# Gate logits of a token's own row: from nine rows by tokens, turned, to tokens by nine columns

## The chip, the cores and the metric

The kernel runs on one core of a Trainium2 chip, as one launch. The metric is device time in microseconds (us). Three runs of the kernel before gave 445.64, 446.63 and 454.53 us, median 446.63 us.

## The reference

The input x has 128 sequences of 64 tokens with 128 channels, so 8192 tokens. Two residual blocks are computed:

```
x = x + tanh(g_xattn) * attention(layernorm(x), ctx, ctx)     # 16 heads of 8, softmax over 64 keys, W_o
x = x + tanh(g_ffn)   * experts(layernorm(x))                 # top 1 of 8 experts
experts(y): logits = (y @ w_red) @ normalised(wg).T           # [tokens, 8]
            idx = argmax, score = max of softmax(logits)
            o = (gelu(y @ W1[idx] + b1[idx]) @ W2[idx] + b2[idx]) * score
```

The kernel does not wait for the finished attention to compute the logits from it. Layer normalisation is linear in the row apart from its scale, and so the logits of a token are the sum of a share of its own row (the subject of the change) and a share of the attention's output, times a scale. With `wc`, a matrix of 128 channels by nine columns (eight experts' weights, mean taken out, and 1/128 for the mean), the own share is xnormed @ wc, times the row's standard deviation.

## The kernel before, in words

**Tiling.** The tokens are cut into 64 units of 128 tokens, and the units into 16 chunks of four. One loop of 76 slots (`for k in range(SLOTS)`, k = 4s + j) is written out on each engine, and each slot serves one unit at each stage of the attention: `scores1` (L1167) for the maximum over keys, four units behind; `scores2` (L1150, L1157) ten behind; values (L1232) eleven behind; the output matrix (L1244) twelve behind. Each slot has also one of four pieces of work on chunk s, by j:

- j = 0: four turns of the normalised x (L1319) and four of the context (L1266), one turn of `xwT` (L1325), one turn of the maxima `mx` (L1327); on ScalarE the copies `xT` (L629), `cT` (L575) and `mS` (L663);
- j = 1: keys (L1273); on VectorE `x_logits`, which scales the own logits into `XR` (L811);
- j = 2: the first two units of `x_logits` on TensorE (L1256), then queries (L1337, 512 columns);
- j = 3: the other two units of L1256, then values of the context (L1344); on ScalarE the copies `V` (L656), and `xwT` (L668).

In the slot k = 7 (s = 1, j = 3) all four units of chunk 0 are done in one L1256 block. The first softmax comes in slot 10.

**The order of the work** is that of the program on each engine, tied by semaphores. A slot's loop runs over three engines: TensorE's `scores1` of unit k - 4 is reduced by VectorE (L1012, in two halves); ScalarE's two exponentials `PT` of slot k (L614, L616) wait for the halves; TensorE's L1150 of the next slot waits for both exponentials (`pt_ok`). GpSimd makes `MD` from `mS` (L459) and then sends finished rows with their logits to a list in HBM by indirect DMAs (L416, 64 of them). SyncE's queue loads x, context and weights and spreads keys and queries.

**The expert part** (from about 299 us) takes 71 tiles of 128 rows from that list, with two layers on TensorE (L1286, L1384) and an indirect DMA by GpSimd for each tile's output (L489).

**The own logits before.** `x_logits` (L1249) multiplies `wc` padded to 32 columns, held stationary, with the 128 turned rows of a unit moving. Unit u of a chunk lands on partitions 32u to 32u + 31 of the PSUM bank `m2`, so the four units of a chunk use four column groups of the array. ScalarE copies the block to `xwT`, TensorE turns it into another part of `m2`, and VectorE reads 8 of each 32 columns with the tokens on the partitions.

Of the kernel before, what the change touches and what calls it, by code (L numbers as in the profile page):

```python
# [6 lines left out]
ACT = mybir.ActivationFunctionType  # L7
# [6 lines left out]
P = 128  # L14
# [6 lines left out]
CU = 4  # L21
CT = CU * P
NC = N // CT
# [5 lines left out]
NE = 8  # L29
# [5 lines left out]
NX = NE + 1  # L35
# [28 lines left out]
def gated_block(nc, x, ctx_in, g_xattn, g_ffn, W_q, b_q, W_k, b_k, W_v, b_v, W_o, b_o, w_red, wg, W1, b1, W2, b2, out):  # L64
    es = ExitStack()
    with es:
        def sb(name, shape, dt=F32):
            return es.enter_context(nc.sbuf_tensor(name, shape, dt))
# [4 lines left out]
        def sem(name):  # L73
            return es.enter_context(nc.semaphore(name))
# [7 lines left out]
        ident = sb("ident", [P, P])  # L82
# [10 lines left out]
        wt = sb("wt", [P, 2, P])  # L93
# [9 lines left out]
        wgT = sb("wgT", [GD, NE])  # L103
        nrm = sb("nrm", [NE, 4])
        wmean = sb("wmean", [GD, 2])
        wc = sb("wc", [P, 32])
        w1 = sb("w1", [P, NE, HID])
        w2 = sb("w2", [P, NE, HH, D])
        w1l = sb("w1l", [P, NE, HID])
# [15 lines left out]
        gve, dev2, bmean = sb("gve", [P, CU]), sb("dev2", [P, D]), sb("bmean", [P, 2])  # L125
        xn = sb("xn", [P, CU, D])
        xT = [sb(f"xT{i}", [P, CT]) for i in range(2)]
        cT, xwT = sb("cT", [P, CT]), sb("xwT", [P, P])
        Qf = sb("Qf", [P, CT])
        qb = [sb(f"qb{i}", [P, CT], BF16) for i in range(2)]  # L130
        kb = sb("kb", [P, CT], BF16)
# [37 lines left out]
        pv = pb("pv", [P, 512])  # L169
        rec = pv[:, 400:416].rearrange("p (a l) -> p a l", l=2)  # L170
        m0, m1, m2 = (pb(n, [P, 512]) for n in ("m0", "m1", "m2"))
# [22 lines left out]
        s1_ps, mxa_ok, mx_ok, mT_ps, mS_ok, s2_ps, pt_ok = (sem(n) for n in ("s1_ps", "mxa_ok", "mx_ok", "mT_ps", "mS_ok", "s2_ps", "pt_ok"))  # L194
        pv_ps, val_ps, tv_ok, rec_ok, nv_ok, ot_ok, x1_ok = (
            sem(n) for n in ("pv_ps", "val_ps", "tv_ok", "rec_ok", "nv_ok", "ot_ok", "x1_ok"))
        gsq_ok, gve_ok, g_pay, xw_ps, xwT_ok, xwt_ps, lgx_ok = (
            sem(n) for n in ("gsq_ok", "gve_ok", "g_pay", "xw_ps", "xwT_ok", "xwt_ps", "lgx_ok"))
        wt_ps, wt_ok, woc_ps, wox_ok, std_ok, peak_ok, lead_ok = (
            sem(n) for n in ("wt_ps", "wt_ok", "woc_ps", "wox_ok", "std_ok", "peak_ok", "lead_ok"))  # L200
        diff_ok, ex_ok, oh_ok, cnt_ps, cnt_rd, pos_ok, gate_ok = (
# [292 lines left out]
        def _(act):  # L494
# [110 lines left out]
            for k in range(SLOTS):  # L605
                s, j = k // CU, k % CU
                n = k - LAG2
                if 0 <= n < NU:
                    act.wait_ge(s2_ps, n + 1)
                    act.wait_ge(mxa_ok, min(k - LAG1 + 1, NU))  # L610
                    if n >= 2:
                        act.wait_ge(pv_ps, pv_turn(n - 2 + LAGV))
                    pt = PT[n % 2][:, :, :].rearrange("p (t i) q -> p t (i q)", t=RT)
                    nc.scalar.activation(pt[:, 0:2], sc[:, 0:2, 256:512], ACT.Exp)  # L614
                    act.wait_ge(mx_ok, min(k - LAG1 + 1, NU))
                    nc.scalar.activation(pt[:, 2:4], sc[:, 2:4, 256:512], ACT.Exp).then_inc(pt_ok, 1)  # L616
                if k == 7:
                    gate_weights_end()
                if k == 0:
                    turned_context(0)  # L620
                    permuted(wq, wqp)
                    permuted_biases()
                    bias_columns()
                    keys(0)
                if j == 0 and s < NC:
                    act.wait_ge(xT_ps, s + 1)
                    if s >= 2:
                        act.wait_ge(xw_ps, s - 1)
                    nc.scalar.activation(xT[s % 2][:, :], m0[:, :], ACT.Copy).then_inc(xT_sb, 1)  # L629
                if k == 0:  # L630
                    keys_turned(0)
                    act.wait_ge(w_in, 16 * NWI)
                    nc.scalar.activation(tg[:, :], gx[:, :], ACT.Tanh)
                    nc.scalar.activation(tgf[:, :], gf[:, :], ACT.Tanh).then_inc(tg_ok, 1)
                if j == 0 and 1 <= s < NC:
                    turned_context(s)
                if j == 1 and 1 <= s < NC:
                    keys(s)
                    keys_turned(s)
                if j == 2 and s < NC:  # L640
                    act.wait_ge(q_ps, s + 1)
                    if s >= 2:
                        act.wait_ge(s1_ps, CU * (s - 1))
                    nc.scalar.activation(qb[s % 2][:, :], m0[:, :], ACT.Identity, bias=b16[:, 0:1], scale=ISC).then_inc(qb_ok, 1)
                    if s >= 1:
                        act.wait_ge(qd_in[(s - 1) % 3], 16 * HI * ((s - 1) // 3 + 1))
                    nc.scalar.activation(Qf[:, :], m0[:, :], ACT.Identity, bias=b16[:, 0:1], scale=ISC).then_inc(qf_ok, 1)
                if j == 3 and s < NC:
                    act.wait_ge(v_ps, s + 1)
                    if s < 3:  # L650
                        act.wait_ge(zero_p, s + 1)
                    else:
                        act.wait_ge(pv_ps, pv_turn(CU * (s - 3) + CU - 1 + LAGV))
                    for p in range(2):
                        r = slice(S * p, S * p + S)
                        i = nc.scalar.activation(V[s % 3][r, :, :, DK * p:DK * p + DK].rearrange("p u h d -> p (u h) d"),  # L656
                                                 m1[r, :].rearrange("p (a d) -> p a d", d=DK), ACT.Copy)
                    i.then_inc(v_ok, 1)
                if j == 0 and 2 <= s < NC + 2:
                    act.wait_ge(mT_ps, s - 1)  # L660
                    if s >= 4:
                        act.wait_ge(md_ok, s - 3)
                    nc.scalar.activation(mS[s % 2][:, :], m2[:, 0:P], ACT.Copy, scale=-1.0).then_inc(mS_ok, 1)  # L663
                if j == 3 and 1 <= s < NC + 1:
                    act.wait_ge(xw_ps, s)
                    if s >= 2:
                        act.wait_ge(xwt_ps, s - 1)
                    nc.scalar.activation(xwT[:, :], m2[:, P:2 * P], ACT.Copy).then_inc(xwT_ok, 1)  # L668
                if k == 5:
                    reduced_weights()  # L670
                if k == 6:
                    turned_weights()
                if k == 10:
                    output_logits()
                if k - LAGO - 1 >= 0:
                    squares(k - LAGO - 1)
                if k in gate_at:
                    gate_exp(gate_at[k])
                if k == SLOTS - 3:
                    nc.scalar.activation(warm[:, :], one[:, :], ACT.Gelu)  # L680
                if k == SLOTS - 3:
                    f_turned(0)
                if k == SLOTS - 2:
                    f_gelu(0)
                    f_turned(1)
# [11 lines left out]
        def _(dve):  # L697
# [14 lines left out]
            nc.vector.memset(mx[0][:, :, :], 0.0)  # L712
            nc.vector.memset(mx[1][:, :, :], 0.0)
            nc.vector.memset(nrm[:, 3:4], 0.5)
            nc.vector.memset(wc[:, NX:32], 0.0)
            nc.vector.memset(wc[:, NE:NX], 1.0 / D)
            for i in range(2):
                nc.vector.memset(fx[i][:, D - 1:D], 1.0)
# [86 lines left out]

            def x_logits(c):

                dve.wait_ge(xwt_ps, c + 1)
                dve.wait_ge(mS_ok, c + 1)
                dve.wait_ge(std_ok, c + 1)  # L810
                nc.vector.tensor_tensor(XR[:, CU * c:CU * c + CU, D:D + NE],  # L811
                                        m2[:, 2 * P:3 * P].rearrange("p (u r) -> p u r", u=CU)[:, :, 0:NE],
                                        std[c % 3][:, :].rearrange("p (u o) -> p u o", o=1).to_broadcast([P, CU, NE]),
                                        ALU.mult).then_inc(lgx_ok, 1)

# [291 lines left out]
        def _(pe):  # L1107
# [23 lines left out]
            def setup_logits():  # L1131
                pe.wait_ge(wt_ok, 1)
                pe.wait_ge(wc_ok, 1)
                for a in range(2):
                    i = nc.tensor.matmul(pv[:, NX * a:NX * a + NX], wt[:, a, :], wc[:, 0:NX], start=True, stop=True,
                                         skip_group_check=True)
                i.then_inc(woc_ps, 1)

# [110 lines left out]
            def x_logits(c, units):  # L1249

                pe.wait_ge(xT_sb, c + 1)
                pe.wait_ge(wc_ok, 1)
                if c >= 1:
                    pe.wait_ge(lgx_ok, c)
                for u in units:
                    i = nc.tensor.matmul(m2[32 * u:32 * u + 32, P:2 * P], wc[:, :], xT[c % 2][:, P * u:P * u + P],  # L1256
                                         start=True, stop=True, skip_group_check=True)
                if CU - 1 in units:
                    i.then_inc(xw_ps, 1)
# [32 lines left out]
            for k in range(SLOTS):  # L1292
# [28 lines left out]
                    if s >= 1:  # L1321
                        context(s)
                if j == 0 and 2 <= s < NC + 2:
                    pe.wait_ge(xwT_ok, s - 1)
                    nc.tensor.transpose(m2[:, 2 * P:3 * P], xwT[:, :], ident[:, :]).then_inc(xwt_ps, 1)  # L1325
                    pe.wait_ge(mx_ok, CU * (s - 1))
                    nc.tensor.transpose(m2[:, 0:P], mx[s % 2][:, :, :].rearrange("p t r -> p (t r)"),  # L1327
                                        ident[:, :]).then_inc(mT_ps, 1)
# [99 lines left out]
```

## Time and profile before

| | |
|---|---|
| median of 3 runs | 446.63 us |
| lowest, highest | 445.64, 454.53 us |
| span of the profiled execution | 445.2 us, 15463 instructions |
| TensorE matmul busy | 354.6 us (80%), 5630 |
| TensorE weight loads busy | 257.0 us (58%), 5630 |
| VectorE busy | 288.0 us (65%), 1031 |
| ScalarE busy | 241.2 us (54%), 604 |
| GpSimd busy | 260.1 us (58%), 413 |
| mean granted TensorE clock | 0.897 of 2.4 GHz |

The profiled execution has no time of its own beside its span; the span lies 0.4 us under the lowest run and 1.4 us under the median. In the profile PE is TensorE's matmuls, PEld its weight loads, DVE is VectorE, ACT ScalarE, POOL GpSimd. L1256 is line 1256 of the kernel. "issue" is idle time in which the engine waited for nothing that the profile shows, and "remote" is a wait whose releaser it doesn't find.

### The profile page before, as it was taken

Reading aid. Unit: us, or ns where it says so; the run is one execution under the profiler, and the core shown is the slowest. Engines: PE = TensorE matmul, PEld = TensorE weight load, DVE = VectorE, ACT = ScalarE, POOL = GpSimd, SP = SyncE. Lnnn points to the kernel's source line nnn. Section 1 sums busy time; section 2 is a strip of 40 time slices with the busy share of each in tenths; the row PEclk is TensorE's granted clock in tenths of the full one; section 3 lists DMA queues with packets and bytes.
Section 4 is the critical chain, followed back from the end, with each engine's and each line's share of the span. In section 5 each row is a group of like instructions: output and inputs, shape, how many; then the busy total and the mean of one; then the engine's idle time right before and its main releaser. Section 6 shows DMA issues by size and latency. Waiting matters only on the chain.

```text
span 445.2 us, 15463 instructions
## 1 busy us (share of the span) xinstructions
PE 354.6 (80%) x5630; PEld 257.0 (58%) x5630; DVE 288.0 (65%) x1031; ACT 241.2 (54%) x604; POOL 260.1 (58%) x413
## 2 busy tenths in 40 slices
PE   4778999999979889889876776768559888878880
PEld 2346566676636556566543545557448667766770
DVE  6968798989848766868853657565435454445440
ACT  3667889888938676777762524443212333333330
POOL 6558465556866945865854444446564656556652
PEclk9989999999969897998995967579685999999997
DMA  5245444333232131221110111401134222222110
GB/s 124 86 134 132 114 122 121 110 99 106 73 93 77 58 100 35 93 76 35 52 54 28 45 35 49 113 28 41 51 98 115 84 83 81 79 69 77 49 36 4
DMA packets 47157, 34.01 MB, mean 76 GB/s; under 512 B 9800, under 2 KB 42955, under 8 KB 47083
## 3 DMA queue, kind: packets, MB, share of 16 engines
q1 hardware_dynamic: 42440, 23.90, 19.5%
q0 software_dynamic: 4352, 9.00, 6.0%
q8 instruction: 46, 0.75, 0.7%
q14 instruction: 27, 0.22, 0.2%
q10 hardware_dynamic: 292, 0.13, 0.1%
HBM read 17.13 MB, written 10.04 MB: 61 GB/s over the span
## 4 chain that ended last, share of the span: by engine, by line
PE 59%; DVE 14%; issue 12%; ACT 4%; another core or an unknown queue 4%; SPq 2%; DMA 1%; POOL 1%; DVEq 1%; POOLq 0%; ACTq 0%
PE sc L1286 10%; PE m L1384 8%; PE pv L1232 8%; PE sc L1157 5%; PE pv L1244 4%; PE m L1337 4%; PE m L1344 3%; PE sc L1167 3%; PE sc L1150 3%; DVE mx L1012 3%; PE m L1256 2%; PE sc L1278 2%; PE m L1381 2%; PE m L1273 2%
## 5 line engine op out<-in xcount | busy, mean ns | idle before, releaser
L1012 DVE TENSOR_REDUCE mx<-sc 128x8 f32<-128x512 f32 x128 | 82.2, 683 | 45.5 <-PE sc L1167 23.6
L489 POOL DMA_INDIRECT out<-fo,rr x71 | 72.0, 1014 | 58.7 <-DVE fo L1083 39.4
L1232 PE MATMUL pv<-PT,V 128*32 128x64 f32 x2048 | 55.7, 233 | 25.0 <-issue 20.0
L416 POOL DMA_INDIRECT records<-XR,pos x64 | 63.4, 990 | 17.0 <-issue 16.8
L1083 DVE SCALAR_TENSOR_TENSOR fo<-m,rr 128x128 f32<-128x128 f32 x71 | 24.8, 350 | 66.3 <-PE m L1384 55.2
L614 ACT ACTIVATE PT<-sc 128x512 f32<-128x512 f32 x64 | 38.1, 596 | 53.3 <-issue 27.5
L1232 PEld LDWEIGHTS pv<-PT,V 128*32 128x32 f32 x2048 | 39.0, 115 | 39.3 <-issue 32.2
L1286 PE MATMUL sc<-fxT,w1s 128*128 128x128 f32 x284 | 50.2, 304 | 5.6 <-DVE w1s L991 3.0
L1384 PE MATMUL m<-w,fgT 128*128 x284 | 52.9, 313 | 0.1
L459 POOL TENSOR_TENSOR MD<-mS,imask 128x256 bf16<-128x256 bf16 x16 | 9.8, 612 | 70.4 <-ACT mS L663 70.4
L602 ACT ACTIVATE fgT<-sc 128x256 f32<-128x256 f32 x71 | 27.2, 383 | 41.7 <-PE sc L1286 29.5
L1286 PEld LDWEIGHTS sc<-fxT,w1s 128*128 128x128 f32 x284 | 41.0, 208 | 11.6 <-issue 7.8
L1157 PE MATMUL sc<-Qd,kT 32*128 32x128 f32 x1024 | 46.3, 288 | 1.2 <-issue 1.2
L596 ACT ACTIVATE fxT<-sc 128x128 f32<-128x128 f32 x70 | 19.4, 277 | 49.8 <-PE sc L1278 25.2
L1384 PEld LDWEIGHTS m<-w,fgT 128*128 128x128 f32 x284 | 40.5, 206 | 2.2 <-issue 0.2
L1157 PEld LDWEIGHTS sc<-Qd,kT 32*128 32x128 f32 x1024 | 39.4, 201 | 2.8 <-issue 2.7
L1021 DVE STREAM_TRANSPOSE TV<-pv 128x256 f32<-128x256 f32 x64 | 28.3, 441 | 18.6 <-remote 13.1
L616 ACT ACTIVATE PT<-sc 128x512 f32<-128x512 f32 x64 | 38.2, 597 | 0.0
L1278 PE MATMUL sc<-ident,fx 128*128 128x128 f32 x70 | 21.4, 306 | 13.3 <-DVE fx L975 9.2
L1244 PE MATMUL pv<-wox,OT 128*128 128x137 f32 x108 | 29.0, 350 | 1.4 <-issue 1.4
L1150 PEld LDWEIGHTS sc<-MD,usel 32*128 32x128 bf16 x256 | 6.5, 92 | 36.7 <-ACT PT L616 23.7
L543 ACT ACTIVATE dev<-XR 128x128 f32<-128x128 f32 x64 | 25.8, 404 | 1.5 <-issue 1.3
(216 smaller groups left out, 735.3 us busy)
## 6 DMA issues: line engine op xcount, KB each, us to landing
rr<-records SPq DMA_DIRECT2D x71, 72.0 KB, 1.9
XC<-in_x SPq DMA_DIRECT2D x16, 256.0 KB
C<-in_ctx SPq DMA_DIRECT2D x16, 256.0 KB
Qd<-Qf SPq DMA_DIRECT2D x64, 64.0 KB
Kd<-kb SPq DMA_DIRECT2D x64, 32.0 KB
w<-in_L_ffn_W SPq DMA_DIRECT2D x16, 128.0 KB, 2.9
out<-fo,rr POOLq DMA_INDIRECT x71
w1l<-in_L_ffn_W SPq DMA_DIRECT2D x8, 128.0 KB, 3.9
```

What stands on the lines that cost most here:

```text
L416: nc.gpsimd.indirect_dma_start(out=records, out_offset=bass.IndirectOffsetOnAxis(ap=pos[:, u:u + 1], axis=0), in_=XR[:, u, :], in_offset=N ...
L489: nc.gpsimd.indirect_dma_start(out=out_rows, out_offset=bass.IndirectOffsetOnAxis(ap=rr[q][:, R_ID:R_ID + 1].bitcast(U32), axis=0), in_=fo ...
L614: nc.scalar.activation(pt[:, 0:2], sc[:, 0:2, 256:512], ACT.Exp)
L616: nc.scalar.activation(pt[:, 2:4], sc[:, 2:4, 256:512], ACT.Exp).then_inc(pt_ok, 1)
L1012: nc.vector.tensor_reduce(mx[c % 2][:, t:t + 2, HI * u:HI * u + HI], sc[:, t:t + 2, 0:256].rearrange("p t (i k) -> p t i k", i=HI), AX_X, ...
L1021: nc.vector.transpose(TV[:, :, :].rearrange("p a r -> p (a r)"), pv[:, 0:2 * P]).then_inc(tv_ok, 1)
L1157: m = nc.tensor.matmul(sc[:, t, 256 + P * b:256 + P * b + P].rearrange("p (i q) -> p i q", i=2), kT[c % 3][r, u, b, :, :].rearrange("r l k ...
L1232: last = nc.tensor.matmul(pv[32 * t:32 * t + 32, P * b:P * b + P].rearrange("p (h i q) -> p i h q", h=2, i=2)[:, i], vf[:, at:at + 32], PT ...
L1244: last = nc.tensor.matmul(attn_out(k), OT[no % 2][:, :], wox[:, :], start=True, stop=True, skip_group_check=True)
L1278: nc.tensor.transpose(rows_turned(k), fx[k % 2][:, :], ident[:, :]).then_inc(f_tr, 1)
L1286: i = nc.tensor.matmul(sc[:, 2 + p, P * m:P * m + P], w1s[p][:, P * m:P * m + P], fxT[p][:, :], start=True, stop=True, skip_group_check=True)
L1384: i = nc.tensor.matmul(o, fgT[p][:, m, :], w2[:, bass.ds(e, 1), m, :].rearrange("p o c -> p (o c)"), start=False, stop=(m == HH - 1), skip ...
```

## The change

`x_logits` on TensorE swaps the operands: the 128 turned rows of a unit are the stationary operand, and the nine columns of `wc` move. The result has the tokens on the partitions at once, nine columns for each unit, side by side in `m2`. ScalarE's copy to `xwT`, TensorE's turn of it, their two semaphores and the padding of `wc` go. VectorE's `x_logits` reads the new place and waits for the matmuls (`xw_ps`).

```
-        wc = sb("wc", [P, 32])
+        wc = sb("wc", [P, NX])                      # NX = 9
...
-        cT, xwT = sb("cT", [P, CT]), sb("xwT", [P, P])
+        cT = sb("cT", [P, CT])
...
-                if j == 3 and 1 <= s < NC + 1:      # ScalarE
-                    act.wait_ge(xw_ps, s)
-                    if s >= 2:
-                        act.wait_ge(xwt_ps, s - 1)
-                    nc.scalar.activation(xwT[:, :], m2[:, P:2 * P], ACT.Copy).then_inc(xwT_ok, 1)
...
-            nc.vector.memset(wc[:, NX:32], 0.0)
...
-                dve.wait_ge(xwt_ps, c + 1)          # VectorE, x_logits
+                dve.wait_ge(xw_ps, c + 1)
...
-                                        m2[:, 2 * P:3 * P].rearrange("p (u r) -> p u r", u=CU)[:, :, 0:NE],
+                                        m2[:, P:P + CU * NX].rearrange("p (u r) -> p u r", u=CU)[:, :, 0:NE],
...
-                    i = nc.tensor.matmul(m2[32 * u:32 * u + 32, P:2 * P], wc[:, :], xT[c % 2][:, P * u:P * u + P],
+                    i = nc.tensor.matmul(m2[:, P + NX * u:P + NX * u + NX], xT[c % 2][:, P * u:P * u + P], wc[:, :],
                                          start=True, stop=True, skip_group_check=True)
...
-                    pe.wait_ge(xwT_ok, s - 1)       # TensorE, j = 0
-                    nc.tensor.transpose(m2[:, 2 * P:3 * P], xwT[:, :], ident[:, :]).then_inc(xwt_ps, 1)
```

## Rows read from the trace of the kernel before

**Rows 1.** The page's chain that ended last: shares of the span by engine.
```profile
PE 59%; DVE 14%; issue 12%; ACT 4%; another core or an unknown queue 4%; SPq 2%; DMA 1%; POOL 1%; DVEq 1%; POOLq 0%; ACTq 0%
```

**Rows 2.** Two stages: length, busy of PE, PEld, DVE, ACT, POOL, PEclk, DMA, GB/s.
```profile
33.00:122.00 89.00, 85.23 (x2043) 59.68 (x2047) 79.54 (x272) 77.99 (x179) 56.02 (x136) 1.00 0.40 109
122.00:299.00 177.00, 141.43 (x2717) 94.95 (x2714) 118.15 (x421) 101.22 (x245) 103.21 (x156) 0.84 0.20 61
```

**Rows 3.** Waits of TensorE's weight loads: total us, times, longest us.
```profile
PEld pv L1232 <- issue: 32.2, 47, 2.7
PEld sc L1150 <- ACT PT L616: 23.7, 36, 1.8
```

**Rows 4.** Timeline of weight loads, a j = 2 slot: start us, us, what, [idle before].
```profile
73.81 0.30 PEld L1244 LDWEIGHTS pv<-wox,OT 128*128 128x128 f32 x2
74.24 0.14 PEld L1256 LDWEIGHTS m<-xT,wc 128*32 128x32 f32 x4
74.58 0.30 PEld L1337 LDWEIGHTS m<-xT,wqp 128*128 128x128 f32 x2 [0.20 <-issue]
75.64 0.10 PEld L1150 LDWEIGHTS sc<-MD,usel 32*128 32x128 bf16 x4 [0.76 <-ACT PT L616]
```

**Rows 5.** Timeline of VectorE and ScalarE: second exponentials of two slots, one reduction.
```profile
74.95 0.61 ACT L616 ACTIVATE PT<-sc 128x512 f32<-128x512 f32 x1
...
80.05 1.29 DVE L1012 TENSOR_REDUCE mx<-sc 128x8 f32<-128x512 f32 x2 [0.56 <-PE sc L1167]
...
81.37 0.60 ACT L616 ACTIVATE PT<-sc 128x512 f32<-128x512 f32 x1
```

**Rows 6.** Timeline of weight loads, end of a j = 0 slot.
```profile
80.49 0.30 PEld L1244 LDWEIGHTS pv<-wox,OT 128*128 128x128 f32 x2
80.71 0.48 PEld L1319 LDWEIGHTS m<-ident,xn 128*128 128x128 f32 x4
...
81.59 0.14 PEld L1325 LDWEIGHTS m<-ident,xwT 128*128 128x128 f32 x1
81.70 0.14 PEld L1327 LDWEIGHTS m<-ident,mx 128*128 128x128 f32 x1
82.02 0.10 PEld L1150 LDWEIGHTS sc<-MD,usel 32*128 32x128 bf16 x4 [0.18 <-ACT PT L616]
```

**Rows 7.** Timeline of weight loads: two matmuls of nine columns (setup), full clock.
```profile
30.91 0.53 PEld L1135 LDWEIGHTS pv<-wc,wt 128*128 128x128 f32 x4
31.45 0.12 PEld L1167 LDWEIGHTS sc<-Kd,qb 32*64 32x64 bf16 x8
```

**Rows 8.** Timeline of weight loads, a j = 3 slot.
```profile
77.14 0.30 PEld L1244 LDWEIGHTS pv<-wox,OT 128*128 128x128 f32 x2
...
77.91 1.01 PEld L1344 LDWEIGHTS m<-wv,cT 128*64 128x64 f32 x32 [0.20 <-issue]
```

**Rows 9.** Timeline of weight loads in setup at half clock: one-column matmuls.
```profile
9.58 0.92 PEld L1112 LDWEIGHTS m<-one,browp 1*128 1x128 f32 x4 [1.50 <-issue]
10.52 0.50 PEld L1319 LDWEIGHTS m<-ident,xn 128*128 128x128 f32 x3
```

**Rows 10.** Timeline of weight loads in slot 7: four units in one block.
```profile
26.35 0.23 PEld L1256 LDWEIGHTS m<-xT,wc 128*32 128x32 f32 x8 [0.30 <-issue]
26.97 0.40 PEld L1344 LDWEIGHTS m<-wv,cT 128*64 128x64 f32 x6 [0.38 <-issue]
```

**Rows 11.** The chain of waits after slot 7's block: start us, us, what.
```profile
27.04 1.93 PE m L1344 x32
...
29.60 0.60 ACT V L656
```

**Rows 12.** Timeline of ScalarE in two j = 3 slots with a gate's exponential.
```profile
106.81 0.28 ACT L668 ACTIVATE xwT<-m 128x128 f32<-128x128 f32 x1
106.98 0.39 ACT L543 ACTIVATE dev<-XR 128x128 f32<-128x128 f32 x1
...
208.33 0.28 ACT L668 ACTIVATE xwT<-m 128x128 f32<-128x128 f32 x1
```

More of the change, by code:

```diff
@@ L196, in gated_block @@
             sem(n) for n in ("pv_ps", "val_ps", "tv_ok", "rec_ok", "nv_ok", "ot_ok", "x1_ok"))
-        gsq_ok, gve_ok, g_pay, xw_ps, xwT_ok, xwt_ps, lgx_ok = (
-            sem(n) for n in ("gsq_ok", "gve_ok", "g_pay", "xw_ps", "xwT_ok", "xwt_ps", "lgx_ok"))
+        gsq_ok, gve_ok, g_pay, xw_ps, lgx_ok = (sem(n) for n in ("gsq_ok", "gve_ok", "g_pay", "xw_ps", "lgx_ok"))
         wt_ps, wt_ok, woc_ps, wox_ok, std_ok, peak_ok, lead_ok = (
@@ L1134, in setup_logits @@
                 for a in range(2):
-                    i = nc.tensor.matmul(pv[:, NX * a:NX * a + NX], wt[:, a, :], wc[:, 0:NX], start=True, stop=True,
+                    i = nc.tensor.matmul(pv[:, NX * a:NX * a + NX], wt[:, a, :], wc[:, :], start=True, stop=True,
                                          skip_group_check=True)
```

## The prediction, made before the changed kernel was run

> **What bounds the kernel now.** I read the chain of waits first. TensorE holds 59% of it [rows 1], so what the change takes from TensorE and ScalarE counts only where that work ends a wait. Next, the busy time by stage: from 33 to 122 us TensorE computes 85 of 89 us at full clock, and from 122 to 299 us 141 of 177 us at a mean clock of 0.84 [rows 2]. The second stage is long because of the largest wait, in which no engine holds TensorE up: L1232 stands 32.2 us on "issue" [rows 3]. The change has no part in L1232.
>
> Then the waits at the slot's edge. A slot begins with L1150, which waits for the second exponential L616 of the slot before, and in 36 of the 64 slots the weight loads end their idle time on just that [rows 3]. The timeline shows the loop behind it. The reduction takes 1.29 us from 80.05, to 81.34. L616 starts at 81.37 and ends at 81.97 [rows 5], and L1150 loads at 82.02 [rows 6], 0.05 us later. So the j = 0 slot, which holds L1325, ends on VectorE's reduction and one exponential, though TensorE looks full in it. The j = 2 slot is nearly as tight: L616 ends at 75.56 [rows 5], L1150 loads at 75.64 [rows 4]. With a release of 0.05 us, only 0.03 us is left between TensorE's pace and the loop's.
>
> **The change part by part.**
>
> *The block of two units in a j = 2 slot (14 slots, s = 2 to 15).* Counted from L1244's first load. Now L1337 loads at 74.58 - 73.81 = 0.77 us [rows 4]. Of this 0.43 us passes before L1256 loads, while behind the same L1244 a block with the full 128 x 128 tile loads after 80.71 - 80.49 = 0.22 us [rows 6]: passing from a tile of 128 columns to one of 32 costs the difference. The new form is the full tile. Its price is its weight loads: the setup has the same form, two float32 matmuls with 128 x 128 stationary and nine columns moving, and takes 31.45 - 30.91 = 0.54 us for four loads, the passage to another tile included [rows 7]. The pace of 128 x 128 float32 loads is (81.59 - 80.71) / 8 = 0.11 us [rows 6], over four of L1319 and four of L1266. So L1337 would load at 0.22 + 4 x 0.11 = 0.66 us, 0.10 us sooner (0.11 before rounding). But the loop allows 0.03. The bounds are 14 x 0.03 = 0.4 and 14 x 0.10 = 1.4 us; some of these slots end later than the loop wants, behind the holes in L1232, and keep the whole. I take -0.6, near the lower end, since rows 3 put most slot edges on the exponential.
>
> *The block of two units in a j = 3 slot (14 slots).* Now L1344 loads 77.91 - 77.14 = 0.77 us after L1244 [rows 8]. New: 0.22 + 0.54 = 0.76, since L1344 has another tile and the passage stays. I take 0; bounds -0.01 and +0.01 a slot.
>
> *The block of four units in slot 7.* This is where the old form was cheap. Its units lie in four column groups, and eight loads and matmuls pass in 26.97 - 26.35 = 0.62 us, at half clock [rows 10]. The new form has one tile for all and must take eight full loads in turn. At half clock four 128-column loads with one-column matmuls take 10.52 - 9.58 = 0.94 us [rows 9], 0.215 each without the end. Eight are 0.94 + 4 x 0.215 = 1.80 us, so +1.2 us. At full clock it would be 0.54 + 4 x 0.11 - 0.62 = +0.4, the lower bound. It is on the path: L1344, then the copy V (L656), then the context's turns follow it in the chain [rows 11].
> The Trainium skill, in "TensorE: Matmul & The Clock Gate" (Part 3, Packing small matmuls), says that matmuls of 32 output rows in different column groups run at once, three of them 2.38 times as fast; by that rule alone undoing the packing is a loss, as the 0.62 us for eight show here, but the j = 2 and j = 3 blocks had only two groups side by side.
>
> *L1325, the turn.* It takes 81.70 - 81.59 = 0.11 us [rows 6] on TensorE, 16 times. 15 lie in slots that end on the exponential: 0, with a bound of -1.6 us if the loop weren't there. The first lies in the setup on the path between V and slot 10: -0.1.
>
> *L668, ScalarE's copy.* The work behind it starts 106.98 - 106.81 = 0.17 us later [rows 12]. In a usual slot the exponential waits for the reduction anyway: 0. In three slots, from 106.81 to 208.33 us, ScalarE also has a gate's exponential and goes from V to the exponentials without a pause [rows 12], the first and the last of them, so 3 x 0.17 = -0.5.
>
> *VectorE.* `x_logits` reads the same 32 elements a partition, waits for an event that comes a slot earlier, and also for `mS` as before: 0. Behind it stand VectorE's gate steps and the next reduction, which lose nothing. One memset in the setup: 0, it ran beside the first loads. GpSimd's MD waits for `mS`, behind `xT` and `cT` on ScalarE: unmoved, and so are the sends. No DMA is added or moved, on SyncE's queue or GpSimd's.
>
> **Sum:** +1.2 - 0.1 - 0.6 - 0.5 = 0.0 us against the span of 445.2, which lies 1.4 us under the median. The same on the median: **446.6 us**. The profile's best reading of the edit is that it gives back in many slots what it costs once.
>
> **The rivals.**
>
> *TensorE's time counts everywhere.* If the slots are bound by TensorE rather than by the loop (it is 96% busy up to 122 us), the saving is 14 x 0.10 + 16 x 0.11 + 0.5 = 3.7 us; less 1.2 in slot 7 is -2.5, and 444.1 us. For it: the chain's share. Against: L1150's waits [rows 3, 5]. Chance 0.17.
>
> *The holes in the supply move.* L1232 stands 32.2 us on "issue", 47 times [rows 3]. The changed kernel has 32 fewer array instructions and its slots shift against GpSimd's sends. If a third of the holes goes, the time is 446.6 - 10.7 = 436 us; as easily a few are added, to about 452. Nothing in the edit pushes either way. 0.12, of which 0.07 for the side below.
>
> *Slower, by the clock.* The clock is 0.84 in the second stage [rows 2] and at half in slot 7. In slot 7 the array now streams nine columns where it streamed 128. If the return to 2.4 GHz comes later there, L1344 (1.93 us at half clock [rows 11], its loads 1.01 at full [rows 8]), the turns and the first scores take about 1.5 us more: 448 us, chance 0.2. That case decides from slot 7, as soon as the granted clock stays at half beyond L1344's matmuls. If it also drops the mean of the second stage, the price is larger: 177 us at 0.84 hold 177 x 0.16 x 2 = 57 us at half clock; at 0.78 it would be 78, and 21 more at half clock cost at most half of that, 10 us: with the 1.5 us of slot 7 that is 458 us, chance 0.06.
> The skill's page "TensorE: Matmul & The Clock Gate" (Part 1, The HAM clock gate) says that the default clock is the low one and that array activity lifts it, which would count against short matmuls between long loads; whether loads count, it doesn't say and no row here shows.
>
> *The change doesn't do what it says:* both the copy and the turn are gone from the text. What can fail is the load pace, if reading `xT` as stationary stalled behind ScalarE's reads: 28 blocks by one more load of 0.11 are +3.1 us, 449.7. Chance 0.05.
>
> **How the numbers follow.** The forecast of no change has 0.40, the rivals 0.17, 0.12, 0.20, 0.06 and 0.05. The range 439 to 452.5 us takes in the first rival, the small clock case, the load pace, the bounds (-1.4 to +1.2) and the spread of the runs shown, and leaves out a large move of the holes and the large clock case. 2% of 446.6 is 8.9 us, about what can be told from no change here. Beyond it lie only the lower case of the holes (0.07) and a little of the first rival together with it, so faster 0.09; the large clock case and a bad move of the holes, so slower 0.08; within 0.83.
>
> **What would show each step.** In the changed profile: L1256 loads of 128 x 128 at 0.11 us a pace; L1337 loading about 0.66 us after L1244; L1150 of the next slot still 0.05 us after L616 in j = 0 and now in j = 2 slots too; the slot 7 block about 1.8 us long if the clock is at half, and the first L1150 about 1.1 us later; that lag worked off by some 0.3 to 0.4 us until 122 us, and the rest behind it. The sum is wrong if the first L1150 isn't later, if j = 0 slots get shorter, or if the second stage's clock or its "issue" time differs by more than a few us.

## The result, and the profile after

The changed kernel took **453.34 us** (median of 4 runs, 450.57 to 456.07), the kernel before 447.60 beside it (median of 4). The ratio is 1.0145, 95% interval 1.0091 to 1.0199. Timed a second time among the experiments it gave 1.0124 (1.0044 to 1.0203). A ratio here compares only the runs within 1.5% of the fastest of their own kernel. The change is a loss of some 1.3%, 5 to 6 us, where I had forecast none, and 453.34 lies above the range.

One caution first. The two profiles are 8.8 us apart, and that is more than the change. A span is some 2 us shorter than the time of its run (454.0 for 456.07 us). The 77 runs of the kernel before that the ratios below use have a mean time of 447.5 us (443.1 to 450.9) and a mean span of 445.1, so the profile of before, with 445.2, is an ordinary one. The four runs of the changed kernel have a mean span of 451.2 us, and the one profiled, with 454.0, is the longest of them. Some 3 us of the 8.8 are the luck of that run.

The page of the changed kernel, busy time by engine, the clock, and the chain by engine:

```profile
span 454.0 us, 15399 instructions
PE 368.4 (81%) x5614; PEld 279.4 (62%) x5614; DVE 289.7 (64%) x1030; ACT 239.4 (53%) x588; POOL 259.9 (57%) x413
PEclk9968999999965898997995757588585999989896
PE 52%; issue 13%; DVE 12%; ACT 6%; another core or an unknown queue 4%; POOL 1%; DVEq 0%; POOLq 0%; ACTq 0%
```

The 16 copies are gone from ScalarE (588 for 604) and the 16 turns from TensorE (5614 for 5630), as the diff says. Weight loads are busy 22 us longer. The first digits of the clock row are the first surprise: the third and fourth slice are 6 and 8, where they were 8 and 9 before.

The same stages as in [rows 2]: length, busy time of PE, PEld, DVE, ACT and POOL, granted clock, DMA share, GB/s.

```profile
33.00:122.00 89.00, 85.44 (x2011) 62.36 (x2014) 78.56 (x266) 75.64 (x168) 54.84 (x135) 0.98 0.38 104
122.00:299.00 177.00, 146.44 (x2709) 106.09 (x2698) 116.26 (x411) 99.31 (x234) 102.22 (x155) 0.79 0.20 62
```

The second stage runs at 0.79 where it ran at 0.84.

**The steady part went as worked out.** Weight loads of a j = 2, a j = 3 and a j = 0 slot of the changed kernel (L1237 is the old L1244, L1249 the block in question, L1328 and L1335 the old L1337 and L1344, L1143 the old L1150, L1318 the old L1327):

```profile
76.80 0.30 PEld L1237 LDWEIGHTS pv<-wox,OT 128*128 128x128 f32 x2
77.03 0.53 PEld L1249 LDWEIGHTS m<-wc,xT 128*128 128x128 f32 x4
77.48 0.30 PEld L1328 LDWEIGHTS m<-xT,wqp 128*128 128x128 f32 x2
78.60 0.10 PEld L1143 LDWEIGHTS sc<-MD,usel 32*128 32x128 bf16 x4 [0.82 <-ACT PT L615]
...
80.10 0.30 PEld L1237 LDWEIGHTS pv<-wox,OT 128*128 128x128 f32 x2
80.33 0.53 PEld L1249 LDWEIGHTS m<-wc,xT 128*128 128x128 f32 x4
80.88 1.01 PEld L1335 LDWEIGHTS m<-wv,cT 128*64 128x64 f32 x32
81.96 0.10 PEld L1143 LDWEIGHTS sc<-MD,usel 32*128 32x128 bf16 x4
...
84.56 0.14 PEld L1318 LDWEIGHTS m<-ident,mx 128*128 128x128 f32 x1
84.99 0.10 PEld L1143 LDWEIGHTS sc<-MD,usel 32*128 32x128 bf16 x4 [0.28 <-ACT PT L615]
```

L1328 loads 0.68 us after L1237 (0.66 forecast, 0.77 in [rows 4]); L1335 0.78 us after (0.76 forecast, 0.77 in [rows 8]). From the L1143 at 78.60 to that at 81.96 are 3.36 us, to the next 3.03. Over the slots 13 to 36 the median j = 0 slot takes 3.03 us before and 3.04 after, the median j = 2 slot 3.34 and 3.30, the median j = 3 slot 3.35 and 3.36. Without the turn the idle time before L1143 is 0.28 us where it was 0.18 in [rows 6], and its releaser is still the exponential: the turn's 0.1 us became a wait.

**The start did not.** Weight loads of the changed kernel from slot 7 to slot 10 (L1160 is the old L1167, L1128 the old L1135):

```profile
26.35 1.78 PEld L1249 LDWEIGHTS m<-wc,xT 128*128 128x128 f32 x8 [0.21 <-issue]
28.16 1.79 PEld L1335 LDWEIGHTS m<-wv,cT 128*64 128x64 f32 x32
...
32.40 0.98 PEld L1128 LDWEIGHTS pv<-wc,wt 128*128 128x128 f32 x4
33.41 0.14 PEld L1160 LDWEIGHTS sc<-Kd,qb 32*64 32x64 bf16 x8
...
35.78 0.11 PEld L1143 LDWEIGHTS sc<-MD,usel 32*128 32x128 bf16 x4 [1.50 <-DVE mx L1005]
```

The block takes 28.16 - 26.35 = 1.81 us, the 1.80 of the forecast, against 0.62 [rows 10]. But the setup block L1128 takes 1.01 us here and 0.54 before [rows 7], so the array is still at half clock, and the first scores load at 35.78 instead of 33.2 us. The granted clock shows it. Windows from 26 us, the same columns, of the kernel before:

```profile
26.00:30.00 4.00, 3.87 (x60) 2.64 (x60) 2.77 (x9) 1.23 (x4) 2.12 (x5) 0.59 0.18 62
30.00:34.00 4.00, 3.31 (x48) 2.23 (x48) 2.78 (x10) 2.86 (x7) 1.11 (x2) 1.00 0.55 132
34.00:38.00 4.00, 3.00 (x74) 1.59 (x68) 3.62 (x10) 3.32 (x8) 4.00 (x11) 1.00 0.86 203
```

and of the changed kernel:

```profile
26.00:30.00 4.00, 3.93 (x48) 3.69 (x48) 2.25 (x8) 0.24 (x2) 2.11 (x5) 0.54 0.21 76
30.00:34.00 4.00, 4.00 (x34) 3.12 (x31) 1.63 (x5) 2.55 (x5) 0.51 (x1) 0.50 0.73 138
34.00:38.00 4.00, 4.00 (x35) 2.04 (x36) 2.58 (x8) 2.06 (x4) 2.52 (x7) 0.68 0.54 149
```

In both profiles the clock has just fallen to 1.2 GHz when the block begins at 26.35 us. Before, it is back at 2.4 GHz (1.00) from 30 us on; after, it stays at 0.50 until beyond 34. TensorE counts as busy in the trace throughout: 3.93 of 4 us, then 4.00 of 4.

**And a collision behind it.** The last of VectorE's five steps on the expert bias, the reduction behind it, GpSimd's constants (the first and the last of a run of 22 memsets), and the exponential that waits, in slot 11 of the changed kernel:

```profile
40.32 2.20 DVE L815 CAST bhl<-br 128x8 bf16<-128x8 f32 x1
40.62 0.22 POOL L430 MEMSET tri<- 128x128 bf16 x1
40.64 1.89 DVE L1005 TENSOR_REDUCE mx<-sc 128x8 f32<-128x512 f32 x2
...
42.38 0.12 POOL L438 MEMSET ebase<- 128x1 f32 x1
42.64 0.60 ACT L613 ACTIVATE PT<-sc 128x512 f32<-128x512 f32 x1 [2.25 <-DVE mx L1005]
```

The cast of eight elements takes 2.20 us and ends at 42.52, with GpSimd's run of memsets. Its siblings take 0.4 us. The two halves of the reduction, which start at 40.64, take 1.89 us where they take 1.27 behind the same cast before, and the exponential L613 starts only at 42.64, behind them. The Trainium skill, in "SBUF — State Buffer" (Terms), says that VectorE and GpSimd arbitrate for one pair of ports, held for a whole instruction, and that the loser blocks; that fits these rows in kind, but the cast here ends with the whole run and not with one memset. The next slot start, 4.6 us after the last, shows the price: the same slot took 3.45 us before. It happened in both profiles of the changed kernel and in that of e9 below, and in no profile in which the clock was back by 34 us.

### The profile page after: what moved, and what is told of

Same layout as the page of the kernel before. It is cut to its first block, busy times and chain, and to the rows that moved or that the text cites. A ratio compares the mean times of both kernels' runs of the same rounds, so it can differ in the third digit from the quotient of the medians.

```text
span 454.0 us, 15399 instructions
## 1 busy us (share of the span) xinstructions
PE 368.4 (81%) x5614; PEld 279.4 (62%) x5614; DVE 289.7 (64%) x1030; ACT 239.4 (53%) x588; POOL 259.9 (57%) x413
## 4 chain that ended last, share of the span: by engine, by line
PE 52%; issue 13%; DVE 12%; ACT 6%; another core or an unknown queue 4%; POOL 1%; DVEq 0%; POOLq 0%; ACTq 0%
PE sc L1279 9%; PE m L1375 7%; PE pv L1225 7%; PE sc L1150 6%; PE m L1335 3%; PE m L1328 3%; PE pv L1237 3%; PE sc L1143 3%; DVE mx L1005 3%; PE sc L1160 3%; PE m L1249 2%; ACT PT L615 2%; ACT PT L613 2%; PE sc L1271 2%
## 5 line engine op out<-in xcount | busy, mean ns | idle before, releaser
L1225 PE MATMUL pv<-PT,V 128*32 128x64 f32 x2048 | 56.8, 240 | 22.6 <-issue 18.3
L613 ACT ACTIVATE PT<-sc 128x512 f32<-128x512 f32 x64 | 38.3, 598 | 57.4 <-issue 28.0
L1225 PEld LDWEIGHTS pv<-PT,V 128*32 128x32 f32 x2048 | 40.6, 120 | 36.8 <-issue 29.4
L1279 PE MATMUL sc<-fxT,w1s 128*128 128x128 f32 x284 | 52.0, 311 | 6.5 <-issue 3.0
L1375 PE MATMUL m<-w,fgT 128*128 x284 | 54.7, 320 | 0.1
L1150 PE MATMUL sc<-Qd,kT 32*128 32x128 f32 x1024 | 49.7, 303 | 1.3 <-issue 1.3
L1279 PEld LDWEIGHTS sc<-fxT,w1s 128*128 128x128 f32 x284 | 42.5, 215 | 12.5 <-issue 7.2
L595 ACT ACTIVATE fxT<-sc 128x128 f32<-128x128 f32 x70 | 19.4, 277 | 49.5 <-PE sc L1271 34.9
L1150 PEld LDWEIGHTS sc<-Qd,kT 32*128 32x128 f32 x1024 | 42.9, 214 | 2.5 <-issue 2.4
L1375 PEld LDWEIGHTS m<-w,fgT 128*128 128x128 f32 x284 | 42.2, 213 | 2.5 <-issue 0.2
L615 ACT ACTIVATE PT<-sc 128x512 f32<-128x512 f32 x64 | 38.2, 597 | 0.0
L1143 PEld LDWEIGHTS sc<-MD,usel 32*128 32x128 bf16 x256 | 6.6, 92 | 38.9 <-ACT PT L615 27.3
L1237 PE MATMUL pv<-wox,OT 128*128 128x137 f32 x108 | 28.8, 350 | 1.3 <-issue 1.3
L1143 PE MATMUL sc<-MD,usel 32*128 32x256 bf16 x256 | 20.0, 302 | 9.4 <-ACT PT L615 7.7
```

Source lines behind the costliest of these rows:

```text
L1143: nc.tensor.matmul(sc[:, t, 256:512].rearrange("p (b i q) -> p i b q", b=2, i=2), usel[r, u, :, :].rearrange("r l k -> r (l k)"), MD[c % 2 ...
L1150: m = nc.tensor.matmul(sc[:, t, 256 + P * b:256 + P * b + P].rearrange("p (i q) -> p i q", i=2), kT[c % 3][r, u, b, :, :].rearrange("r l k ...
L1225: last = nc.tensor.matmul(pv[32 * t:32 * t + 32, P * b:P * b + P].rearrange("p (h i q) -> p i h q", h=2, i=2)[:, i], vf[:, at:at + 32], PT ...
L1237: last = nc.tensor.matmul(attn_out(k), OT[no % 2][:, :], wox[:, :], start=True, stop=True, skip_group_check=True)
L1279: i = nc.tensor.matmul(sc[:, 2 + p, P * m:P * m + P], w1s[p][:, P * m:P * m + P], fxT[p][:, :], start=True, stop=True, skip_group_check=True)
L1375: i = nc.tensor.matmul(o, fgT[p][:, m, :], w2[:, bass.ds(e, 1), m, :].rearrange("p o c -> p (o c)"), start=False, stop=(m == HH - 1), skip ...
```

## The experiments

Each ratio is to runs of the kernel before on the same chip. "Half clock" is the time at 1.2 GHz of a run, (1 - mean granted clock) x 2 x span, meaned over the runs in the ratio; for the kernel before it is 100.6 us at a mean clock of 0.887. The last column gives the mean time of the runs in the ratio and that of all runs (three, of 483, 908 and 1463 us, are in no figure). The ratio is as recorded and not the quotient of these means.

| chunk 0 (slot 7) | other chunks | else | ratio (95%) | half clock, us | mean us, in the ratio / all |
|---|---|---|---|---|---|
| old | old | | 1 | 100.6 | 447.5 / 448.8 |
| new | new, 9 columns | the change | 1.0145 (1.0091 to 1.0199) | 117.1 | 453.3 / 453.3 |
| new | new, 9 | again | 1.0124 (1.0044 to 1.0203) | 114.6 | 453.0 / 455.1 |
| old | new, 9 | e1 | 1.0033 (0.9979 to 1.0087) | 109.5 | 449.1 / 449.1 |
| old | new, 9 | e11 | 0.9995 (0.9947 to 1.0044) | 108.2 | 447.7 / 449.4 |
| new | old | e2 | 1.0069 (1.0026 to 1.0113) | 106.4 | 450.1 / 450.9 |
| new, 96 columns | new, 96 | e3 | 1.0045 (1.0009 to 1.0081) | 103.8 | 449.9 / 449.9 |
| new, 48 | new, 48 | e9 | 1.0065 (1.0022 to 1.0108) | 109.5 | 450.5 / 451.7 |
| old | new, 96 | e6 | 0.9948 (0.9898 to 0.9998) | 96.2 | 444.4 / 447.5 |
| old | new, 96 | e12 | 0.9950 (0.9889 to 1.0010) | 96.0 | 445.6 / 447.6 |
| new | new, 9 | turn and copy kept idle, e8 | 1.0083 (1.0033 to 1.0132) | 107.9 | 451.2 / 452.7 |
| new | new, 9 | split in slot 12, e7 | 1.0007 (0.9965 to 1.0049) | 106.7 | 449.6 / 452.1 |
| new | new, 9 | split in slot 14, e4 | 1.0073 (1.0031 to 1.0115) | 112.7 | 450.8 / 450.8 |
| old | new, 96 | split in slot 12, e10 | 0.9981 (0.9943 to 1.0020) | 104.4 | 447.4 / 447.9 |

**1. The old form in slot 7 alone (e1, and again as e11).** Theory A puts the loss in the start, theory B in the number of columns that the array streams in every chunk. The code here and below is shortened, with numbers in place of names; lines with + and - are against the changed kernel, if nothing else is said.

```
 def x_logits(c, units):
     for u in units:
+        if c == 0:   # column groups, wc padded to 32; ScalarE copies, TensorE turns, for this chunk alone
+            matmul(m2[32 * u:32 * u + 32, P:2 * P], wc[:, 0:32], xT[c % 2][:, P * u:P * u + P])
+        else:
             matmul(m2[:, P + 9 * u:P + 9 * u + 9], xT[c % 2][:, P * u:P * u + P], wc[:, 0:9])
```

> The new form for chunks 1 to 15, the old form (column groups, copy, turn) for chunk 0 alone, so slot 7 has its short block back. Theory A (the loss is the start: slot 7's serial loads and what follows from them): the first softmax slot starts at 33.2 us again, ratio to before 0.997 to 1.002. Theory B (the array streams fewer columns in every chunk and the clock stays low longer in the second stage): the start is regained, 2 to 3 us, but the half-clock time between slots 37 and 73 stays 15 us or more over the 55 of before and the ratio is 1.006 to 1.012.

> The same kernel as in the first experiment (chunk 0 old, chunks 1 to 15 with nine columns), again, on one chip with the next. If the width sets the clock in the steady part: 1.001 to 1.006 and 5 us or more at half clock above the kernel with 96 columns. If not: the two agree in both.

Measured 1.0033 and 0.9995, and in the two profiles the first scores load at 32.86 and 34.21 us. The start is most of the loss: 1.2% goes with one block of one slot. The half-clock time of 108 to 110 us stays 8 to 9 over the kernel before, and in the profiles that between slots 37 and 73 is 63 us where it was 55. Theory B forecast at least 15 us more between those slots. The new form of the other chunks saves nothing that can be seen: 449.1 and 447.7 us are on average 1.0 us over the kernel before.

**2. The new form in slot 7 alone (e2).**

The lines stand against the kernel before, as a sketch.

```
+        if c >= 1:   # as before
             matmul(m2[32 * u:32 * u + 32, P:2 * P], wc[:, 0:32], xT[c % 2][:, P * u:P * u + P])
+        else:
+            matmul(m2[:, P + 9 * u:P + 9 * u + 9], xT[c % 2][:, P * u:P * u + P], wc[:, 0:9])
```

> The kernel before, with the new form in chunk 0 alone. Theory A: nearly the whole loss, 1.008 to 1.014, with the clock returning at 36 us and not at 29. Theory B: only the start's loss, 1.004 to 1.007, second stage as before.

1.0069: the block's 1.2 us alone would be 1.0027, the lower end of the interval. In its profile the clock is at 0.50 from 26 to 30 and 0.52 from 30 to 34 us. This was theory B's figure in my expectation. The start alone costs 2.7 us here (450.1 against 447.5), and less than the 4.7 us that it is worth where the other chunks have nine columns (453.1 against 448.5). The two parts by themselves, 2.7 and 1.0 us, make 3.7 of the 5.7 us of the change. Each of these differences is uncertain by 1 to 2 us.

**3. More columns moving (e3 with 96, e9 with 48).** The stationary operand and the number of loads stay; only the moving operand is wider, and what it adds is never read.

```
-        wc = sb("wc", [P, 9])
+        wc = sb("wc", [P, 96])        # columns 9 to 95: a constant
...
-            matmul(m2[:, P + 9 * u:P + 9 * u + 9], xT[...], wc[:, 0:9])
+            matmul(m2[:, P + 96 * u:P + 96 * u + 96], xT[...], wc[:, 0:96])
```

> The new form in every chunk, but 96 columns move instead of 9 (the other 87 hold a constant and are not read), so the array streams longer behind the same weight loads of 0.11 us. If streaming decides the clock (theory B): half-clock time falls to that of before, the clock returns at 29 us in slot 7, ratio 1.000 to 1.005. If it is the serial loads and the shift of the holes (theory A): no difference to the changed kernel, 1.010 to 1.016.

> The new form with 48 columns moving in every chunk, between 9 (1.0124, clock 0.870) and 96 (1.0045, clock 0.884). If the streamed columns set the clock, it lies between them: clock 0.874 to 0.882, ratio 1.006 to 1.011. If the 96 columns only moved the phase, it is like either end by chance.

Work that nobody reads makes the kernel faster: 1.0045 for 1.0124 and 1.0145 with 96, 1.0065 with 48. Half-clock time goes down with the columns: 115 to 117 us for 9, 109.5 for 48, 103.8 for 96. Start of the kernel with 96 columns, weight loads, and its window from 30 us:

```profile
26.42 1.78 PEld L1268 LDWEIGHTS m<-wc,xT 128*128 128x128 f32 x8 [0.34 <-issue]
28.37 1.79 PEld L1357 LDWEIGHTS m<-wv,cT 128*64 128x64 f32 x32 [0.17 <-issue]
...
32.62 0.53 PEld L1143 LDWEIGHTS pv<-wc,wt 128*128 128x128 f32 x4
33.17 0.12 PEld L1175 LDWEIGHTS sc<-Kd,qb 32*64 32x64 bf16 x8
```

```profile
30.00:34.00 4.00, 4.00 (x38) 2.88 (x35) 2.00 (x5) 2.54 (x5) 0.34 (x1) 0.67 0.50 130
34.00:38.00 4.00, 3.15 (x40) 1.49 (x42) 3.40 (x12) 3.28 (x6) 3.06 (x8) 1.00 0.52 156
```

The block is 0.14 us longer (28.37 - 26.42 = 1.95), yet the setup block takes 0.55 us and the clock is at 1.00 by 34 us, in a profile whose clock fell, like that of the changed kernel, just before the block. The interval of 96 columns lies below that of the changed kernel's first timing and overlaps that of the second, and that of 48 overlaps both. It is the order of both columns of the table, times and clock, with and without the new start, that carries the claim. The one profile does not. In four profiles with nine columns in slot 7 the clock came back nearly as early, at 33.1 (e4), 33.2 (e8), 33.8 (e2) and 34.0 us (e7), and in that with 48 columns only at 37.8. And my expectation for 96 columns, a clock that returns at 29 us, was missed: it is 0.50 from 26 to 30 and back at 32.6. A rival stays, too: every edit of the changed kernel that was timed came out below it, also those that touch no column (e4, e7, e8: 449.6 to 451.2 us for 453.1). So a part of what 96 and 48 columns give back with the new start can be a mere shift of the schedule.

**4. Both costs out (e6, again as e12).**

> Chunk 0 in the old form, chunks 1 to 15 in the new form with 96 columns moving. Both suspected costs are out and the steady saving stays. If streaming sets the clock: clock at or over that of the kernel before (0.882), half-clock time 5 us or more under that of the same kernel with nine columns (109.5 us), ratio 0.995 to 1.001. If width has no part in the clock: the same 1.003 as with nine columns.

> Chunk 0 old, chunks 1 to 15 with 96 columns, again. If its 0.9948 was real: 0.993 to 0.998. If it was the luck of one batch: 0.998 to 1.003.

0.9948 and 0.9950, half-clock time 96 us. This version beats the changed kernel. Over the kernel before it leads by half a percent, at the edge of what its intervals show, and part of that comes from which runs are compared: 11 of its 23 runs lie more than 1.5% over their fastest and drop out of its ratios. Over all runs it takes 447.5 us against 448.8, a lead of 1.2 us, uncertain by 1.5, with about the half-clock time of the kernel before (102.5 against 103.8). That it is the fastest of all is not shown. Stages of the second of these kernels (as in the changed kernel's rows above):

```profile
15.00:33.00 18.00, 13.52 (x182) 8.55 (x178) 14.90 (x52) 11.22 (x26) 10.41 (x25) 1.00 0.37 118
33.00:124.00 91.00, 86.19 (x2044) 63.07 (x2036) 80.39 (x270) 77.36 (x174) 58.25 (x139) 1.00 0.40 113
```

In this profile the clock never left 2.4 GHz in the start; the block of slot 7 took 0.39 us and the first scores loaded at 32.1 us.

The four corners, from the means of the runs in the ratios: with the new start 453.1 us (9 columns) and 449.9 (96); with the old start 448.5 and 445.0. By these the start is worth 4.7 to 4.9 us and the width 3.2 to 3.5 us. Over all runs the corners are 454.4, 449.9, 449.3 and 447.5: the start 2.4 to 5.1 us, the width 1.8 to 4.5. Both have the same sign throughout, and their sizes are known only roughly. With 96 columns the median j = 3 slot takes 3.43 to 3.44 us and not 3.36, so the width costs 0.08 us in 14 slots and gives back more.

**5. The turn and the copy kept as idle work (e8).**

```
     # ScalarE, j == 3
+    activation(xwT[:, :], ident[:, :], ACT.Copy)
     # TensorE, j == 0
+    transpose(m2[:, 2 * P:3 * P], mx[s % 2], ident)
     transpose(m2[:, 0:P], mx[s % 2], ident)
```

> The changed kernel with the removed ScalarE copy and TensorE turn put back as idle work of the same size at the same places (the copy reads the identity, the turn reads the maxima; nothing uses them). My claim is that both are hidden in the loop: ratio 1.012 to 1.015, at most 1 us over the changed kernel. If the turn's streaming holds the clock up: clock 0.875 or more and 1.008 or less.

1.0083: no slower, if anything faster, than without them. End of a j = 0 slot in this kernel (L1341 is the added turn):

```profile
82.95 0.14 PEld L1341 LDWEIGHTS m<-ident,mx 128*128 128x128 f32 x1
83.06 0.14 PEld L1342 LDWEIGHTS m<-ident,mx 128*128 128x128 f32 x1
83.54 0.10 PEld L1159 LDWEIGHTS sc<-MD,usel 32*128 32x128 bf16 x4 [0.34 <-ACT PT L618]
```

The turn is hidden: L1159 still waits for the exponential behind both turns. That the copy is hidden too, as it was put back here, is not shown: the j = 0 slots 16 to 28 take 3.19 to 3.20 us in this profile and 3.03 to 3.04 in those of both kernels. So the run does not put back exactly what the change took out. Whether the turn's streaming also holds the clock up is not settled. The mean clock of 0.880 meets my figure for it (0.875 or more), the ratio misses that for it (1.008 or less) by 0.0003, and 451.2 us against 453.1 lies within the noise.

**6. The split elsewhere (e7 and e4 in the changed kernel, e10 with 96 columns).**

```
-                if k == 10:
+                if k == 12:          # e4: 14
                     split_biases()
```

> The changed kernel with VectorE's split of the expert bias in slot 12 instead of slot 10, behind GpSimd's memsets. In both profiles of the changed kernel its last cast takes 2.2 us (0.4 before) and ends with those memsets. Theory C (that collision is a steady part of the loss): every cast 0.4 us or less, slot 11 at 3.4 to 3.5 us instead of 4.6, ratio 1.008 to 1.011 against 1.0124. Rival (the softmax loop takes it up again, or it is only in these profiles): 1.011 to 1.015.

> The kernel before with VectorE's split of the expert bias moved from slot 10 to slot 14, away from GpSimd's constants. It tells what the split costs before the change: theory C (in the changed kernel the split's cast of 2.2 us, 0.4 before, waits for GpSimd's memsets since VectorE lags and GpSimd doesn't) says that here it is 0.4 a cast in slot 14 as well, slot 11 is shorter by 0.3 to 0.5 us, ratio 0.997 to 1.001.

> Chunk 0 in the old form, the rest with 96 columns, and the split in slot 12. If the split's place matters for itself: 0.991 to 0.995, under the 0.9948 without it. If it mattered only through the collision, which this start doesn't have: 0.994 to 0.998.

The kernel that ran as e4 is not the one that its expectation describes. It has the new form in every chunk, and differs from e7 in the slot of the split alone. Its page has 5614 matmuls and 588 instructions on ScalarE, as that of the changed kernel, and its slot 7 has the new block:

```profile
28.05 0.97 PEld L1267 LDWEIGHTS m<-wc,xT 128*128 128x128 f32 x8 [1.15 <-issue]
```

So no run tells what the split's place costs in the kernel before, and its ratio of 1.0073 can't be held against 0.997 to 1.001. It is a second run of theory C in the changed kernel, where the figure was 1.008 to 1.011.

In e7 the casts take 0.13 to 0.17 us and in e4 0.14 to 0.41, none of them 2.2, and slot 11 takes 3.55 us in both where it took 4.63 with the collision. The ratios are 1.0007 and 1.0073, both under the changed kernel's 1.0124 and 1.0145. The mean times are 449.6 and 450.8 us, 3.5 and 2.3 under the 453.1 of the changed kernel, each uncertain by some 2 us, and over all runs 2.3 and 3.6 under. (The ratio of e7 looks better than its times: 449.6 against 447.6 us on its chip would be 1.0045.) So theory C fits: the collision is a part of the loss, 0.8 to 1.1 us by its slot in the three profiles. Whether it is more can't be told; the half-clock time of e7 is 8 to 10 us lower as well and that of e4 2 to 4. In e10, where nothing collides, the same move gave 0.9981 for 0.9948 and 0.9950, and 447.9 for 447.5 us over all runs: moving the split is no gain by itself, as the second half of my expectation had it.

**7. The changed kernel again (e5).**

> The changed kernel itself, timed again beside the two forms of slot 7 and of the width. If start and clock each hold about half of the loss: 1.009 to 1.013, mean granted clock 0.868 to 0.874 against 0.88 to 0.885 of the kernel before, 8 to 14 us more at half clock. If the first four runs were only unlucky: 1.004 to 1.008 with a clock like that of the kernel before.

1.0124. In its profile the clock is at 0.50 from 30 to 38 us, and the cast takes 2.20 us again.

## Why the prediction was wrong, step by step

**The sum's slot 7 term was mis-sized.** "+1.2 us" is what the block costs: measured 1.81 - 0.62 = 1.2. But I ended the term there and put what follows into a rival of 0.20, "the small clock case". It is what happens. Over the eight profiles with the new form in slot 7 the first scores start at 34.9 to 37.0 us, mean 35.8; over the six with the old form at 32.1 to 34.2, mean 33.2. That is 2.6 us by slot 10, and 3.5 us by slot 37 (124.4 against 120.9). The recorded clock is at half before the first scores for 10.2 us on average (6.8 to 13.7) against 3.4 (0 to 6.8). In the timed runs the start is worth 2.7 us (e2) to 4.9.

**The rival's own price was right only in part.** I gave the clock in slot 7 1.5 us over the 1.2, which is 2.7, and 2.6 was measured at the first scores in the profile shown. I left out that a late TensorE and VectorE meet a GpSimd that isn't late: the collision, another 0.8 to 1.1 us in slot 11 of three profiles. And even this rival's total, 448 us, lies 5 us under what was measured.

**"Neutral in a j = 3 slot, -0.03 to -0.10 in a j = 2 slot" held** at full clock: L1328 and L1335 load at 0.68 and 0.78 us for 0.66 and 0.76, the median slots changed by -0.04 and +0.01 us, and the slot edge is now set by L615. **"The turn: 0" held**: 3.04 us for 3.03 in the median j = 0 slot. **"The copy: -0.5"** can't be told apart from the rest. The three together were to save about 1.1 us, and e1 and e11, which have them without the new start, are 1.0 us slower than the kernel before, uncertain by 1.1.

**The sum had no term for the clock outside slot 7.** I had it only as "if it also drops the mean of the second stage", with 0.06. With the old start, where only the steady form differs, the runs in the ratios have 8 to 9 us more at half clock with nine columns than the kernel before, and 4 to 5 less with 96; over all runs 6 more and 1 less. That nine columns go with more time at half clock than 96 holds either way (by 13 and by 8 us). That 96 go with less than the kernel before does not. Among the runs of one kernel 1 us more at half clock goes with 0.16 us more time (the 77 of the kernel before) to 0.20 (the twelve experiments, each about its own mean). By that estimate 13 us are 2.1 to 2.6 us of the 3.5 that the width is worth with the old start. The row that I leaned on for cheapness, "two matmuls with nine columns take 0.54 us for four loads", says how long the array is held and nothing of the clock.

The Trainium skill, in "TensorE: Matmul & The Clock Gate" (Part 1, The HAM clock gate), says that the low clock is the default and activity lifts it. I cited it and gave it too small a chance. Read by the trace's busy row, that did not come out here: the granted clock was 0.50 from 30 to 34 us while TensorE counted as busy for 4.00 of 4 us. Why, no run shows.

**The base was off by 1 us:** I forecast on a median of three, 446.6, and the kernel's mean over the 77 runs is 447.5. The case "within 2%", with 0.83, did come: 1.3% is less. The range and the time did not.

What stays open: how the start's share divides between the block's length, the clock and the collision; what the split's place does in the kernel before, which no run has; why nine columns go with more time at half clock; and whether the removed turn had a part in it. The expert part and the holes before L1232 (29.4 us of "issue" at L1225 after, for 32.2 in [rows 3]) were not touched by any run.

## What to carry to other kernels

Before swapping operands so that few columns move behind full weight loads, look at what it does to the granted clock, and not only at how long the array is held. Here the kernels with nine columns spent more time at half clock than those with 96, and 87 columns that nobody reads, at 0.08 us a slot, more than paid for themselves. Look at the one place where the old form was at its best, here four column groups at once in a start at half clock, and price that place by itself, with the clock of that moment and with what a later arrival will meet. Work taken out of a slot that ends on another engine's loop was worth nothing here (the turn, 3.03 us a slot with it and 3.04 without); check that by who releases the next slot's first instruction, not by how full the engine looks.

## What the runs showed of the hardware that I had not expected

A VectorE cast of eight elements a partition took 2.20 us instead of 0.40 where GpSimd's run of 22 memsets began 0.3 us after it, and it ended 0.02 us after the last memset's end in the row above (42.38 + 0.12). It came in three profiles, each with the clock low until 36 us or later.

The time at half clock of one kernel differs much from run to run: in six profiles with the old slot 7, the start spent between 0 and 6.8 us at 1.2 GHz with the same instructions up to slot 7. A single profile of such a kernel can't carry a claim of 1%.
